# The preparation as pieces of the batches' list schedule, in smaller splits, with the weight sums and a mask on POOL and x among the first loads

## The chip, the cores and the metric

The kernel runs on one core of a Trainium2 chip. Its engines are PE (matrix products and transposes, into PSUM banks), ACT, DVE and POOL (elementwise work) and SP (here only issuing DMAs). Each has its own queue of instructions, carried out in order, and they wait for each other by semaphores. The metric is the device time of the whole program in microseconds.

## What is computed

x is 16 batches of 512 rows and 256 features, adj is one 512x512 matrix for all. Four layers follow one another, each with a residual and a layernorm:

```python
x = _layernorm(x + _L0_gnn_ref(...))   # norm_adj @ (x @ weight); norm_adj = adj scaled by rsqrt(degree) on both sides
x = _layernorm(x + _L1_gnn_ref(...))   # attention, 8 heads, masked where adj == 0; proj; o + layernorm(o)
x = _layernorm(x + _L2_gnn_ref(...))   # 3 steps of a gated unit on adj @ h
x = _layernorm(x + _L3_gnn_ref(...))   # attention, 8 heads, scores + (1 - adj) * -1e9; proj
```

float32 throughout; only the weights, adj and vectors that depend on no batch can be prepared ahead.

## The kernel before

Each float32 operand of a product is held as a high part, rounded to fp32r (ACT writes it), and a low part, the remainder (DVE or POOL writes it); a product is three matmuls on PE, high x low, high x high and low x high (L1226 to L1228, `product`). adj is used transposed (`adjT`), all weights lie in one tensor `W` (HI, LO), of which the first nine blocks of 256 columns ("plain": w0, q1, k1, v1, o1, q3, k3, v3, o3) come straight from memory by way of `raw`, and five ("turned": w3, w4, w5, u3, u5) must be transposed by PE first. w3, w4 and w5 are sums of two halves, w4 has w3 subtracted from it, q1 and q3 are scaled.

Three batches are in flight (`STREAMS`), each with its own buffers `res`, `vh`, `feat`, `qk`. One attention runs at a time, in tiles of 128 queries: scores on PE (L1275), mask and least value on DVE (L1031, `shift`), exponential on ACT (L805), transposes on PE (L1283), a copy to `PT` by ACT or DVE, values on PE (L1298). For it the parts of q and k are copied to `stack` by DMAs (L676).

The order on every engine comes from a planner at build time, the class `Order`: each piece of work has an engine, an assumed duration and lateness (`nominal`), the pieces it comes after, and the PSUM banks that it opens or frees. `run` takes again and again, among the heads of all its queues, the piece with the earliest start, and of equals the one with the longest way to the end (`ways`). The result is one fixed order for each engine, `order.by_engine`; on the chip every engine goes through its own and waits where it must, whatever the planner had assumed.

The preparation is not in that plan: it is written out at the head of each engine's program. SP issues adj, then w3, w4, w5, u3, u5, then the plain weights, then rows and vectors, all of these on one semaphore `raw_loaded`. DVE (L934 to L973) computes the degrees, mask1 (bf16) and mask3 (float32), the low parts of adjT, and after `raw_loaded` the scalings and sums, the bias columns, dinv (the power itself is POOL's, L691), bo, the low part of all plain weights in one instruction (L967) and five low parts of the turned ones (L971). ACT writes the high parts, the plain ones in one instruction (L783). PE transposes adj (L1207), and after DVE's u5 the five weights (L1215), then a small product for bo (L1219). SP waits for the last low part, stores bo to memory (L642), waits for that, and only then takes up the planned order, in which the loads of x for batches 0, 1 and 2 (L658) and the bias row (L653) come first. `raw` lies over `feat` and `qk`, the buffers of the batches; raw w3 and w4 lie in `PT`, w5 in `vh2`, u3 and u5 in `res2`.

A batch then goes: x scaled by dinv (high L833 on ACT, low L1070 on DVE), POOL adds the bias row (L738), two products with adjT ("ax"), two with w0, layernorm n0 (moments on DVE, power on POOL L704, ACT L840), transposes (L1266), q, k, v, stack, attention.

## Time and profile before

| what | us |
|---|---|
| median of 3 runs | 2619.9 |
| lowest and highest | 2617.76, 2620.14 |
| the profiled execution, time | 2621.08 |
| its span in the trace | 2619.3 |

The mean granted clock of PE in the profiled execution was 0.989 of full speed. "Busy" counts the instructions' own time; what an engine stands still for is named as the releaser in brackets. A row of the timeline gives start, duration, engine, line and operation, with neighbours of one kind merged (x4).

### The profile page before, as it was taken

Reading aid. Unit: us, or ns where it says so; the run is one execution under the profiler, and the core shown is the slowest. Engines: PE = TensorE matmul, PEld = TensorE weight load, DVE = VectorE, ACT = ScalarE, POOL = GpSimd, SP = SyncE. Lnnn points to the kernel's source line nnn. Section 1 sums busy time; section 2 is a strip of 40 time slices with the busy share of each in tenths; the row PEclk is TensorE's granted clock in tenths of the full one; section 3 lists DMA queues with packets and bytes.
Section 4 is the critical chain, followed back from the end, with each engine's and each line's share of the span. In section 5 each row is a group of like instructions: output and inputs, shape, how many; then the busy total and the mean of one; then the engine's idle time right before and its main releaser. Section 6 shows DMA issues by size and latency. Waiting matters only on the chain.

```text
span 2619.3 us, 50145 instructions
## 1 busy us (share of the span) xinstructions
PE 2544.9 (97%) x17384; PEld 2048.2 (78%) x17384; DVE 1973.5 (75%) x5487; ACT 1896.5 (72%) x4273; POOL 756.2 (29%) x1081
## 2 busy tenths in 40 slices
PE   4999999999999999999999999999999999999997
PEld 3877777887878888787887878888788887778875
DVE  4867867868687786887868788786887868776776
ACT  3767857769587695867769587695877859575787
POOL 1222242322413223142322413224142232323221
PEclk7999999999999999999999999999999999999999
DMA  3312203122031221302122031221212223021122
GB/s 117 73 27 49 52 20 69 32 61 60 26 70 42 53 51 45 73 22 65 38 54 67 21 76 41 53 52 45 66 29 55 48 51 69 19 51 27 31 63 54
DMA packets 91082, 132.14 MB, mean 50 GB/s; under 512 B 15921, under 2 KB 40146, under 8 KB 90834
## 3 DMA queue, kind: packets, MB, share of 16 engines
q1 hardware_dynamic: 90834, 128.94, 20.7%
q8 instruction: 143, 2.34, 0.4%
q14 instruction: 105, 0.86, 0.1%
HBM read 19.83 MB, written 8.39 MB: 11 GB/s over the span
## 4 chain that ended last, share of the span: by engine, by line
PE 91%; DVE 4%; issue 1%; ACT 1%; POOL 1%; SPq 1%; DMA 0%; DVEq 0%; ACTq 0%; POOLq 0%
PE bank L1226 18%; PE bank L1227 17%; PE bank L1228 17%; PE bank L1283 16%; PE bank L1298 9%; PE bank L1275 8%; PE bank L1303 2%; PE bank L1266 2%; PE bank L1336 1%; DVE probs L1031 1%; SPq L624 1%; DVE vh L1097 0%; ACT probs L805 0%; DVE gate L1008 0%; DVE gate L1132 0%
## 5 line engine op out<-in xcount | busy, mean ns | idle before, releaser
L805 ACT ACTIVATE probs<-probs,few 128x512 f32<-128x512 f32 x1024 | 732.5, 720 | 88.8 <-DVE few L1031 84.4
L1031 DVE CUSTOM_DVE_ANT_0 probs<-bank,mask 128x512 f32<-128x512 f32 x1024 | 677.3, 683 | 58.3 <-PE bank L1283 26.3
L1283 PE MATMUL bank<-ident,probs 128*128 128x128 f32 x4096 | 585.4, 273 | 8.9 <-ACT probs L805 7.1
L1283 PEld LDWEIGHTS bank<-ident,probs 128*128 128x128 f32 x4096 | 484.1, 141 | 92.8 <-issue 27.9
L1275 PE MATMUL bank<-stack 96*128 96x512 f32 x1024 | 415.2, 451 | 1.8 <-DMA stack<-qk 0.7
L814 ACT ACTIVATE PT<-bank 128x512 f32<-128x512 f32 x630 | 354.6, 597 | 51.3 <-PE bank L1303 25.8
L1042 DVE COPY PT<-bank 128x512 f32<-128x512 f32 x394 | 269.0, 688 | 84.7 <-PE bank L1283 46.4
L727 POOL TENSOR_TENSOR feat<-o,feat 128x256 fp32r<-128x256 f32 x128 | 95.2, 744 | 615.1 <-ACT feat L827 606.3
L1226 PE MATMUL bank<-feat,W 128*128 128x512 f32 x640 | 259.9, 406 | 0.0
L1298 PE MATMUL bank<-PT,vh 128*32 128x256 f32 x4096 | 254.8, 383 | 1.1 <-issue 0.7
L840 ACT ACTIVATE res<-res,few 128x256 f32<-128x256 f32 x256 | 139.6, 593 | 156.8 <-POOL few L712 155.0
L1227 PE MATMUL bank<-feat,W 128*128 128x512 f32 x640 | 252.9, 395 | 0.0
L1228 PE MATMUL bank<-feat,W 128*128 128x512 f32 x640 | 252.8, 395 | 0.0
L1226 PE MATMUL bank<-qk,W 128*128 128x512 f32 x576 | 231.3, 402 | 2.9 <-DVE few L1031 1.9
L1226 PE MATMUL bank<-adjT,qk 128*128 128x512 f32 x512 | 208.6, 407 | 24.3 <-DVE qk L1070 15.7
L1228 PE MATMUL bank<-qk,W 128*128 128x512 f32 x576 | 227.7, 395 | 0.0
L1227 PE MATMUL bank<-qk,W 128*128 128x512 f32 x576 | 227.5, 395 | 0.0
L744 POOL TENSOR_TENSOR feat<-gate,feat 128x512 fp32r<-128x512 f32 x96 | 130.1, 1368 | 277.8 <-ACT feat L868 277.7
L1227 PE MATMUL bank<-adjT,qk 128*128 128x512 f32 x512 | 204.8, 400 | 0.0
L1228 PE MATMUL bank<-adjT,qk 128*128 128x512 f32 x512 | 204.2, 399 | 0.0
L794 ACT ACTIVATE qk<-bank 128x512 fp32r<-128x512 f32 x160 | 94.6, 593 | 146.4 <-PE bank L1228 146.3
L805 ACT ACTIVATION_READ_ACCUMULATOR probs<-probs,few 128x1 f32 x1024 | 198.7, 194 | 0.0
(110 smaller groups left out, 4995.6 us busy)
## 6 DMA issues: line engine op xcount, KB each, us to landing
stack<-qk SPq DMA_DIRECT2D x768, 128.0 KB, 2.4
res<-in_x_dram SPq DMA_DIRECT2D x16, 512.0 KB, 3.8
out_dram<-res SPq DMA_DIRECT2D x16, 512.0 KB, 2.9
rows<-bo_sum SPq DMA_DIRECT2D x15, 128.0 KB, 2.9
rows<-in_L_gnn_bias_dram SPq DMA_DIRECT2D x14, 128.0 KB, 2.9
rows<-in_L_gnn_ln_beta_dram SPq DMA_DIRECT2D x14, 128.0 KB, 2.9
PT<-in_adj_dram SPq DMA_DIRECT2D x1, 1024.0 KB, 5.4
PT<-in_L_gnn_w_w_dram SPq DMA_DIRECT2D x2, 512.0 KB, 6.7
```

The costliest lines, as they stand in the source:

```text
L744: i = pool.tensor_tensor(feat[j][:, LO, f, :], src[j][:, f, :], feat[j][:, HI, f, :].bitcast(F32), ALU.subtract)
L805: k = act.activation(p, p, ACT.Exp, bias=least[:, t % P_RING:t % P_RING + 1], scale=-1.0, accum_out=sums[:, grp % 2, q * HG + h:q * HG + h ...
L814: k = act.activation(PT[:, t % PT_RING, :], place("transpose", t)[:, :], ACT.Copy)
L840: k = act.activation(res[j][:, t, :], res[j][:, t, :], ACT.Identity, bias=mv[j][:, t, 0:1], scale=mv[j][:, t, 1:2])
L1031: k = dve.tensor_tensor_reduce(out=probs[:, t % P_RING, :], in0=place("scores", t)[:, :], in1=mask[:, half * QT + q, :], scale=1.0, scalar ...
L1042: k = dve.tensor_copy(PT[:, t % PT_RING, :], place("transpose", t)[:, :])
L1226: pe.matmul(dst, a(HI), b(LO), start=start, stop=False)
L1227: pe.matmul(dst, a(HI), b(HI), start=False, stop=False)
L1228: return pe.matmul(dst, a(LO), b(HI), start=False, stop=stop)
L1275: k = pe.matmul(place("scores", t)[:, :], stack[0:STACKED * HD, 0, h, cs], stack[0:STACKED * HD, 1, h, :], start=True, stop=True)
L1283: k = pe.transpose(place("transpose", t)[:, m * P:(m + 1) * P], probs[:, t % P_RING, m * P:(m + 1) * P], ident[:, :])
L1298: pe.matmul(dst[h * HD:(h + 1) * HD, 0:QH], v_v[j][:, m, c:c + HD], pt_v[:, pt_slots(grp, h), m, :], start=(m == 0), stop=(m == NT - 1))
```

## The change

The preparation becomes pieces of the same plan. New planner entries `("raw", ...)` are SP's loads, each group on a semaphore of its own, in the order adj, x of batch 0, w0, x of batch 1, qkv, the other plain weights, the GRU weights, small vectors, rows; `("prep", engine, ...)` are the steps on PE, ACT, DVE and POOL. The plain weights are split in seven pieces for ACT and DVE. The four sums of weights go from DVE to POOL, as does mask3, which comes after the power. The transposes open PSUM banks as other pieces do. `raw` now lies over `stack` and the head of `PT`, adj one slot further in `PT`, raw w4 in `vh1`. x of batch 2 is loaded once u3 and u5 are transposed (they lie in `res2`). The first stack of batch 0 waits for the whole preparation. The arithmetic is the same.

```diff
+PREP_US = {"deg": 2.65, "mask1": 1.14, "mask3": 5.0, "w3": 1.3, "w4": 1.3, "w4-w3": 1.3, "w5": 1.3, "dinv": 0.1, "pow": 0.8, "q1": 0.34, "q3": 0.34, "u5": 0.35,
+           "cols": 0.6, "bv": 0.6, "bo": 0.35, "hi_qkv1": 1.35, "lo_qkv1": 1.65,
+           "lo_q3": 0.6, "hi_q3": 0.5, "bo_sum": 0.1}
+RAW_US = {"adj": (0.6, 4.6), "w0": (0.6, 2.5), "rows": (1.2, 2.0), "qkv1": (0.6, 3.5), "gru": (3.0, 5.0), "rest": (3.0, 5.0),
+          "small": (5.4, 2.0), "bo_sum": (0.6, 3.0)}
+
...
+    turned = ("w3", "w4", "w5", "u3", "u5")
+    adjs = [f"adj{m}" for m in range(NT)]
+    for name in ("adj", "x0", "w0", "x1", "qkv1", "rest", "gru", "small", "rows"):
+        add("first", "SP", ("load", int(name[1])) if name[0] == "x" else ("raw", name))
+    add("bo_sum", "SP", ("raw", "bo_sum"), ("prep", "DVE", "bo"))
+    for m in range(NT):
+        add(("prep", "PE"), "PE", ("prep", "PE", adjs[m]), ("raw", "adj"), opens=[("adjT", m)])
+        add(("prep", "ACT"), "ACT", ("prep", "ACT", adjs[m]), ("prep", "PE", adjs[m]))
+        add(("prep", "DVE"), "DVE", ("prep", "DVE", adjs[m]), ("prep", "ACT", adjs[m]), frees=[("adjT", m)])
+    add("degrees", "DVE", ("prep", "DVE", "deg"), ("raw", "adj"))
+    add("degrees", "POOL", ("prep", "POOL", "pow"), ("prep", "DVE", "deg"))
+    add("degrees", "DVE", ("prep", "DVE", "dinv"), ("prep", "POOL", "pow"))
+    add("masks", "DVE", ("prep", "DVE", "mask1"), ("raw", "adj"))
+    add("masks_pool", "POOL", ("prep", "POOL", "mask3"), ("prep", "POOL", "pow"))
+    later = ("o1", "q3", "k3", "v3", "o3")
+    for loaded, scaled, name in (("w0", None, "w0"), ("qkv1", "q1", "qkv1"),
+                                 *(("rest", "q3" if name == "q3" else None, name) for name in later)):
+        if scaled:
+            add("plain", "DVE", ("prep", "DVE", scaled), ("raw", loaded))
+        add("plain", "ACT", ("prep", "ACT", f"hi_{name}"), ("raw", loaded), *([("prep", "DVE", scaled)] if scaled else []))
+        add("plain", "DVE", ("prep", "DVE", f"lo_{name}"), ("prep", "ACT", f"hi_{name}"))
+    for name in ("w3", "w4", "w4-w3", "w5"):
+        add("sums", "POOL", ("prep", "POOL", name), ("raw", "gru"))
+    add("sums_dve", "DVE", ("prep", "DVE", "u5"), ("raw", "gru"))
+    for name, ready in zip(turned, (("prep", "POOL", "w3"), ("prep", "POOL", "w4-w3"), ("prep", "POOL", "w5"), ("raw", "gru"),
+                                    ("prep", "DVE", "u5"))):
+        add("turned", "PE", ("prep", "PE", name), ready, opens=[("turn", name)])
+        add(("turned", "ACT"), "ACT", ("prep", "ACT", name), ("prep", "PE", name))
+        add(("turned", "DVE"), "DVE", ("prep", "DVE", f"lo_{name}"), ("prep", "ACT", name), frees=[("turn", name)])
+    add("biases", "DVE", ("prep", "DVE", "cols"), ("raw", "small"), ("raw", "rows"))
+    add("biases", "PE", ("prep", "PE", "bv"), ("raw", "small"), ("raw", "rest"), opens=[("bv", 0)])
+    add("biases", "DVE", ("prep", "DVE", "bo"), ("prep", "PE", "bv"), frees=[("bv", 0)])
+    prepared = [("prep", "DVE", name) for name in ("lo_w0", "lo_qkv1", *(f"lo_{name}" for name in later), "lo_u5", "mask1",
+                                                     "dinv", adjs[-1])]
+    prepared += [("prep", "POOL", "mask3"), ("raw", "bo_sum")]
+
     for n, (what, of) in enumerate(ROWS):
-        add("rows", "SP", ("row", n), *([("pool", ROWS[n - 1][0], b) for b in ROWS[n - 1][1]] if n else []))
+        add("rows", "SP", ("row", n), *([("pool", ROWS[n - 1][0], b) for b in ROWS[n - 1][1]] if n else [("raw", "w0")]),
+            *([("raw", "bo_sum")] if what == "bo" else []))
...
-        add(sp, "SP", ("load", b), *([("store", b - STREAMS)] if b >= STREAMS else []))
+        if b >= 2:
+            add(sp, "SP", ("load", b), ("store", b - STREAMS) if b >= STREAMS else ("prep", "PE", "u5"))
         for t in range(NT):
-            add(act, "ACT", ("act", "scale", b, t), ("load", b))
+            add(act, "ACT", ("act", "scale", b, t), ("load", b), ("prep", "DVE", "dinv"))
             add(dve, "DVE", ("dve", "scale", b, t), ("act", "scale", b, t))
         add(pool, "POOL", ("pool", "scale", b), ("dve", "scale", b, NT - 1), ("row", row_at["scale", b]))
         for f in range(FT):
-            add(pe, "PE", ("pe", "ax", b, f), ("dve", "scale", b, NT - 1), opens=[("ax", b, f)])
+            add(pe, "PE", ("pe", "ax", b, f), ("dve", "scale", b, NT - 1), ("prep", "DVE", adjs[-1]), opens=[("ax", b, f)])
             evacuated(b, ("ax", b), f)
...
-            add(pe, "PE", ("pe", "w0", b, tp), ("dve", "ax", b, FT - 1), opens=[("w0", b, tp)])
+            add(pe, "PE", ("pe", "w0", b, tp), ("dve", "ax", b, FT - 1), ("prep", "DVE", "lo_w0"),
+                opens=[("w0", b, tp)])
...
+                        *(prepared if layer == 1 and b == 0 else []), *([("stt", last_of_head(first, h))] if first else []))
...
+                add(pe, "PE", ("pe", "v", b, layer, tp), ("prep", "PE", "w4"), ("prep", "PE", "w5"), opens=[("v", b, layer, tp)])
...
+        raw = nc.alloc_sbuf_tensor_at("raw", [P, FT, PLAIN], F32, offset=at)
         early = PT[:, :, :].rearrange("p r c -> p (r c)")
-        adj_n = early[:, 0:NT * N].rearrange("p (t m) -> p t m", t=NT)
-        raw_w = [v.rearrange("p (o c) -> p o c", o=FT)
-                 for v in (early[:, 4 * N:6 * N], early[:, 6 * N:8 * N], vh[2][:, :])]
+        adj_n = early[:, N:(1 + NT) * N].rearrange("p (t m) -> p t m", t=NT)
+        raw_w = [v.rearrange("p (o c) -> p o c", o=FT) for v in (early[:, 5 * N:7 * N], vh[1][:, :], vh[2][:, :])]
...
+            def raw_loads(what):
+                if what == "adj":
+                    sp.dma_start(adj_n, adj.rearrange("(t p) m -> p t m", p=P)).then_inc(adj_loaded, 16)
+                elif what == "w0":
+                    weights([("w0", w0)], w0_loaded)
+                elif what == "qkv1":
+                    weights([("q1", wqkv)], qkv1_loaded)
+                elif what == "rest":
+                    weights([("o1", wproj), ("q3", wq), ("k3", wk), ("v3", wv), ("o3", wo)], rest_loaded)
+                elif what == "gru":
+                    for to, w in zip(raw_w, (w3, w4, w5)):
+                        sp.dma_start(to, w.rearrange("(o p) c -> p o c", p=P)).then_inc(gru_loaded, 16)
+                    for to, w in zip(raw_u, (u3, u5)):
+                        sp.dma_start(to, w.rearrange("(o p) c -> p o c", p=P)).then_inc(gru_loaded, 16)
+                elif what == "rows":
+                    for i, v in enumerate((gamma, bproj)):
+                        sp.dma_start(rows[:, 1 + i, :], v.partition_broadcast(P)).then_inc(rows_loaded, 16)
+                elif what == "bo_sum":
+                    sp.wait_ge(prep_dve.sem, prep_dve.at("bo"))
+                    sp.dma_start(bo_sum[:, :], raw_bo[0:1, :]).then_inc(bo_stored, 16)
+                else:
+                    sp.dma_start(raw_bo, bo.partition_broadcast(HD)).then_inc(small_loaded, 16)
+                    small(cols, (bq, bk, w3b, w4b, w5b), small_loaded)
+                    small(raw_cols, (u3b, u5b, bv), small_loaded)
...
+                    if n == 2:
+                        sp.wait_ge(bo_stored, 16)
...
+                    if b == 2:
+
+                        wait_full(sp, "turn", "u3")
+                        wait_full(sp, "turn", "u5")
...
+                    if layer == 1 and b == 0:
+
+                        sp.wait_ge(prep_dve.sem, len(prep_dve.steps))
+                        sp.wait_ge(prep_pool.sem, len(prep_pool.steps))
+                        sp.wait_ge(bo_stored, 16)
...
+            def weight_sums(what):
+                pool.wait_ge(gru_loaded, 16 * 5)
+                if what == "w4-w3":
+
+                    pool.wait_ge(prep_pool.sem, prep_pool.at("w4"))
+                    i = pool.tensor_tensor(raw_w[1][:, :, 0:D], raw_w[1][:, :, 0:D], raw_w[0][:, :, 0:D], ALU.subtract)
+                else:
+                    w = raw_w[turned.index(what)]
+                    i = pool.tensor_tensor(w[:, :, 0:D], w[:, :, 0:D], w[:, :, D:2 * D], ALU.add)
+                prep_pool.raised_by(i, what)
+
+            def third_mask():
+                pool.wait_ge(adj_loaded, 16)
+                i = pool.tensor_scalar(mask3[:, :, :], adj_n, 1.0, -FAR, ALU.subtract, ALU.mult)
+                prep_pool.raised_by(i, "mask3")
+
+            def powers():
+                pool.wait_ge(prep_dve.sem, prep_dve.at("some"))
+                prep_pool.raised_by(pool.tensor_tensor(deg[:, 2, :], deg[:, 1, :], power[:, :], ALU.pow), "pow")
...
+            def prepare(what):
+                if what in adjs:
+                    m = adjs.index(what)
+                    wait_full(act, "adjT", m)
+                    k = act.activation(adjT[:, HI, m, :], place("adjT", m)[:, :], ACT.Copy)
+                elif what in turned:
+                    wait_full(act, "turn", what)
+                    c = col[what]
+                    k = act.activation(W[:, HI, :, c:c + D], place("turn", what)[:, :].rearrange("p (k c) -> p k c", k=FT),
+                                       ACT.Copy)
+                else:
+                    if what == "hi_w0":
+                        act.wait_ge(w0_loaded, 16)
+                    elif what == "hi_qkv1":
+                        act.wait_ge(qkv1_loaded, 16)
+                        act.wait_ge(prep_dve.sem, prep_dve.at("q1"))
+                    else:
+                        act.wait_ge(rest_loaded, 16 * 5)
+                        if what == "hi_q3":
+                            act.wait_ge(prep_dve.sem, prep_dve.at("q3"))
+                    c = plain[what[3:]]
+                    k = act.activation(W[:, HI, :, c], raw[:, :, c], ACT.Copy)
+                prep_act.raised_by(k, what)
...
+                elif what in ("q1", "q3"):
+                    if what == "q1":
+                        dve.wait_ge(qkv1_loaded, 16)
+                    else:
+                        dve.wait_ge(rest_loaded, 16 * 5)
+                    c = col[what]
+                    prep(dve.tensor_scalar(raw[:, :, c:c + D], raw[:, :, c:c + D], -SCALE, None, ALU.mult), what)
+                elif what[:3] == "lo_" and what[3:] in plain:
+                    dve.wait_ge(prep_act.sem, prep_act.at("hi" + what[2:]))
+                    c = plain[what[3:]]
+                    prep(dve.tensor_tensor(W[:, LO, :, c], raw[:, :, c], W[:, HI, :, c].bitcast(F32), ALU.subtract), what)
+                elif what == "u5":
+                    dve.wait_ge(gru_loaded, 16 * 5)
+                    prep(dve.tensor_scalar(raw_u[1], raw_u[1], 0.5, None, ALU.mult), what)
...
+                    wait_free(pe, "turn", what)
+                    if what == "u3":
+                        pe.wait_ge(gru_loaded, 16 * 5)
+                    elif what == "u5":
+                        pe.wait_ge(prep_dve.sem, prep_dve.at("u5"))
+                    else:
+                        pe.wait_ge(prep_pool.sem, prep_pool.at("w4-w3" if what == "w4" else what))
...
+                    if f == 0 and b < STREAMS:
+                        pe.wait_ge(prep_dve.sem, prep_dve.all(adjs))
...
```

## Rows read from the trace of the kernel before

**Rows 1.** Busy time, share of span and instructions, the page's first part.

```profile
PE 2544.9 (97%) x17384; PEld 2048.2 (78%) x17384; DVE 1973.5 (75%) x5487; ACT 1896.5 (72%) x4273; POOL 756.2 (29%) x1081
```

**Rows 2.** Stretches: length, busy us (instructions) by engine, granted clock, DMA share, GB/s.

```profile
0.00:46.70 46.70, 9.92 (x40) 7.96 (x41) 21.12 (x33) 12.30 (x15) 2.98 (x9) 0.68 0.47 149
46.70:78.80 32.10, 32.09 (x173) 27.71 (x174) 19.04 (x53) 13.88 (x28) 15.00 (x20) 0.93 0.17 45
...
120.00:300.00 180.00, 170.49 (x1160) 132.35 (x1159) 131.68 (x382) 135.21 (x311) 49.97 (x72) 1.00 0.20 44
300.00:2500.00 2200.00, 2188.46 (x14836) 1766.37 (x14836) 1676.87 (x4627) 1609.23 (x3615) 653.55 (x917) 1.00 0.20 48
2500.00:2619.30 119.30, 102.78 (x846) 80.01 (x844) 89.09 (x285) 90.94 (x220) 27.70 (x53) 0.95 0.23 58
```

The busy columns of such a row are PE, PE's weight loads, DVE, ACT and POOL.

**Rows 3.** Timeline of the preparation: start, duration, engine, line, operation.

```profile
6.19 2.29 DVE L934 TENSOR_REDUCE probs<-PT 128x4 f32<-128x2048 f32 x1 [6.19 <-DMA PT<-in_adj_dram]
...
6.30 3.65 PE L1207 MATMUL bank<-ident,PT 128*128 128x128 f32 x16 [6.30 <-DMA PT<-in_adj_dram]
...
8.84 2.22 POOL L691 TENSOR_TENSOR probs<-probs,few 128x4 f32<-128x4 f32 x1 [7.30 <-DVE probs L937]
...
9.80 1.22 DVE L939 TENSOR_SCALAR mask<-PT 128x2048 f32<-128x2048 f32 x1
...
21.19 0.76 DVE L947 TENSOR_SCALAR raw<-raw 128x512 f32<-128x512 f32 x2 [7.78 <-DMA probs<-in_L_gnn_bv_dram]
...
31.40 4.94 DVE L967 TENSOR_TENSOR W<-raw,W 128x4608 fp32r<-128x4608 f32 x1
...
46.71 0.76 PE L1226 MATMUL bank<-adjT,qk 128*128 128x512 f32 x1 [15.68 <-DVE qk L1070]
```

**Rows 4.** Wo's load: its issue (timeline), and the median from issue to landing.

```profile
9.97 1.08 SPq L624 DMA_DIRECT2D raw<-in_L_gnn_Wo_dram  x1
...
raw<-in_L_gnn_Wo_dram SPq DMA_DIRECT2D x1, 256.0 KB, 8.2
```

**Rows 5.** POOL's groups by line and shape: busy us, mean ns of one.

```profile
L738 POOL TENSOR_TENSOR res<-res,rows 128x1024 f32<-128x1024 f32 x48 | 115.5, 2407 | 233.7 <-DVE feat L998 139.2 <-DVE qk L1070 58.7 <-DMA rows<-in_L_gnn_bias_dram 35.7
L744 POOL TENSOR_TENSOR feat<-vh,feat 128x512 fp32r<-128x512 f32 x64 | 81.9, 1300 | 119.7 <-ACT feat L890 118.8
...
L704 POOL TENSOR_TENSOR few<-few 128x2 f32<-128x2 f32 x160 | 118.8, 743 | 2.7
```

**Rows 6.** DVE beside POOL: two timeline rows, then two lines' min/median/max ns.

```profile
48.59 0.80 DVE L1070 SCALAR_TENSOR_TENSOR qk<-res,few,qk 128x256 fp32r<-128x256 f32 x1 [2.03 <-ACT qk L833]
...
46.74 2.37 POOL L738 TENSOR_TENSOR res<-res,rows 128x1024 f32<-128x1024 f32 x1 [35.68 <-DMA rows<-in_L_gnn_bias_dram]
...
L1070 DVE SCALAR_TENSOR_TENSOR qk<-res,few,qk x64: 450/484/799, 44.9 to 2271.0; 128x256 fp32r<-128x256 f32 x64
...
L1123 DVE SCALAR_TENSOR_TENSOR gate<-gate,vh x96: 640/683/2895, 169.8 to 2507.6; 128x512 f32<-128x512 f32 x96
```

**Rows 7.** Clock: two stretches (columns as Rows 2), and ACT's second evacuation (timeline).

```profile
26.00:28.00 2.00, 2.00 (x11) 2.00 (x10) 0.00 (x0) 1.50 (x4) 0.00 (x0) 0.50 0.00 0
...
51.00:52.00 1.00, 1.00 (x5) 0.78 (x5) 1.00 (x4) 1.00 (x4) 0.00 (x0) 0.86 0.00 0
...
54.65 0.60 ACT L794 ACTIVATE feat<-bank 128x512 fp32r<-128x512 f32 x1 [1.85 <-PE bank L1228]
```

**Rows 8.** From w0 of batch 0 to the first scores, timeline of SP and PE.

```profile
57.55 0.35 SPq L653 DMA_DIRECT2D rows<-in_L_gnn_ln_beta_dram  x1
...
59.94 0.28 PE L1228 MATMUL bank<-W,feat 128*128 128x256 f32 x1
...
65.66 1.03 PE L1266 MATMUL bank<-ident,res 128*128 128x128 f32 x8
...
73.68 50.61 SPq L676 DMA_DIRECT2D stack<-qk  x36
...
78.53 0.71 PE L1275 MATMUL bank<-stack 96*128 96x512 f32 x2
```

More of the change, by code:

```diff
@@ L38, in at, with all @@
         return it * len(self.steps) + self.place[step] + 1
+    def all(self, steps):
+        return max(self.at(step) for step in steps)
     def raised_by(self, instruction, step):
@@ new lines, in weights, with small @@
+            def weights(names, loaded):
+                for name, w in names:
+                    c = col[name]
+                    sp.dma_start(raw[:, :, c:c + w.shape[1]], w.rearrange("(k p) c -> p k c", p=P)).then_inc(loaded, 16)
+            def small(to, vectors, loaded):
+                for i, v in enumerate(vectors):
+                    sp.dma_start(to[:, i, :], v.rearrange("(f p) -> p f", p=P),
+                                 allow_slow_non_contiguous=True).then_inc(loaded, 16)
+            def raw_loads(what):
[22 more added lines that the diff above has]
+                    small(raw_cols, (u3b, u5b, bv), small_loaded)
```

218 lines of the change are left out of this document (108 added, 110 removed).

## The prediction

> **What bounds the kernel now.** Read the busy totals first [rows 1]: PE is busy 97% of the span, DVE 75%, ACT 72%, POOL 29%. So this is a PE kernel, and only time in which PE has nothing to do, or runs at the low clock, can be had. Then read where that time lies [rows 2]. Of the 2619.3 us, PE is busy 2544.9, so it idles 74.4. The first 46.7 us hold 36.8 of them (46.70 − 9.92). The stretch to 78.8 us holds none, 120 to 300 holds 9.5, the 2200 us up to 2500 hold only 11.5, and the last 119 us 16.5. Half of all idle time is the preparation, in 2% of the span. The timeline of the preparation shows why [rows 3]: everything is in series. PE turns adj (6.30, 3.65 us) and is done; DVE waits until 21.19 for the last of 23 small and large loads, SP's single semaphore standing at the very last vector; then it scales and sums the weights, PE turns them, DVE writes the low parts (31.40, 4.94 us, then five pieces). Only then does SP issue the store of bo and, behind it, the first load of x; the first real product starts at 46.71. From there PE is without a gap to the first scores at 78.53 [rows 2, 8].
>
> **The change, part by part.**
>
> *Loads.* adj still lands at 6.2 us. In the kernel before, 4.25 MB more had landed when Wo's load ended, about 8.2 us after its issue at 9.97, so at 18.2 us [rows 4]: 4.25/12.0 = 0.354 MB/us. In the new order (adj, x0, w0, x1, qkv, the rest, the five GRU weights, the first bias row) that rate gives x0 (0.5 MB) at 7.6, w0 (0.25) at 8.3, x1 at 9.7, qkv (0.75) at 11.8, the rest (1.25) at 15.3, the GRU weights (2.0) at 21, the row (0.13) at 21.4. The row's place behind the GRU weights follows from the planner's ranks: when SP comes free at its 6.0, the loads' chain (the weights' and then the small vectors' way) is longer than the row's.
>
> *First product.* The planner believes w0 loaded at its 4.3 us and adj at 5.2, so it puts hi_w0 first on ACT and lo_w0 first on DVE. On the chip adj is there at 6.2 and w0 at 8.3: the degree sum waits behind lo_w0. hi_w0 8.3 to 8.95 (0.60, as ACT's other 128x512 pieces [rows 7]), lo_w0 to 9.7 (0.68, as DVE's median for that size [rows 6]), sum to 12.0 (2.29) and two small steps to 12.2 [rows 3]. The low parts of adjT, 0.68 each, go on; POOL's power took 2.22 us, but ended as DVE's mask3 did, at 11.06 against 11.02; elsewhere the same kind is 0.74 [rows 3, 5]. I take 0.8: power at 13.1. dinv follows the third adjT piece, at 14.3. The fourth piece (0.68) and q1 (0.4, half of the 0.76 at 21.19) take DVE to 15.4, then come the low parts of x0, four in 1.7 (from 44.9 to the product's 46.71 in before [rows 3, 6]), which ACT's parts run ahead of; undisturbed they end at 17.1, and at 17.2 the product starts, 29.5 us earlier than now.
>
> *mask3 on POOL.* This is what disturbs it. Nothing of this shape and operation is on POOL in the trace. From above: a sum of two tensors, 128x1024, takes 2.40, twice that is 4.8 [rows 5]. From below: DVE's own 1.22. I take 4.8, the nearest row being an elementwise POOL operation of half the size. It then runs 13.1 to 17.9. What matters is who waits for it. A DVE operation with two SBUF tensors that meets a POOL one is stretched: the low part of x starting at 48.59 took 0.80 instead of 0.484 while POOL's 46.74 + 2.37 ended at 49.11, and over the kernel one gate operation took 2895 ns where the median is 683 [rows 6]; the excess, 2.2 us, is nearly one POOL operation of 2.40. The power above is the opposite case, POOL held by DVE. So q1 and the low parts of x0 wait until 17.9 and the product starts at 17.9 + 0.4 + 1.7 = 20.0. With the lower price for mask3 it is 17.2.
> The Trainium skill (SBUF — State Buffer, "SBUF: two separate sides") says that VectorE and GpSimd share a port pair as an exclusive lock for a whole instruction, taken by VectorE operations with two SBUF inputs or in a 2-port mode; by that rule reads from PSUM go on. The rows above agree with it. It speaks against moving work from DVE to POOL here: by it the 2.8 us between 17.2 and 20.0 stand, without it the sum would be 2.8 us better.
>
> *PE's ledger.* Idle before: 36.8. Idle after, up to the first product: 6.3 + (20.0 − 9.95) = 16.4 (13.6 with the cheap mask). Clock: all PE work between 20 and 46.7 us, the weight transposes and bv, is 9.92 − 3.65 = 6.3 us at the granted 0.50, the level of 1.2 GHz [rows 2, 3, 7]. Behind products that run at 2.4 GHz it needs half, which gives 3.1 back. The first products of b0 start at the low clock in both kernels (up at 51 to 52, 4.5 us after the start) [rows 7]: no difference. So the ceiling of the gain is 36.8 − 16.4 + 3.1 = 23.5 us, less the new waits.
>
> *New waits of PE, whose queue is fixed.* (a) w3's transposes stand in PE's order behind the two products of b0, which end at 27.9 (from 46.71 to the second one's evacuation at 54.65 it is 7.9 [rows 3, 7]). They need POOL: mask3, then the bias of b0 (2.40, not before its row at 21.4 and not before the low parts of x0), then w3 (1.30) [rows 5]. In clear air that is 25.1; but DVE has q1, x0's parts, mask1, lo_qkv1, u5, x1's parts and more, about 8 us that contend, in one run from 17.9 to 26. POOL gets in late: w3 is ready between 25 and 30. Wait 0 to 2, taken 1.5. (b) w4−w3 and w5 follow 2.6 and 3.9 us later, behind which PE has a product of b1 and w0 of b0: 0 to 2, taken 0.5. (c) b2 can't be loaded before u3 and u5 are turned, at about 38, and so starts at 44; until then PE lives on b0 and b1 alone. In before, nearly six us lie between the end of w0 and the first transposes of n0 (59.94 to 65.66), filled by b1 and b2 [rows 8]. Taken 2, from 0 to 5. (d) DVE: in before it works 21.1 + 19.0 = 40.2 us to 78.8; 4.0 of it go (mask3 1.22, four sums of 0.68), 36 remain between 9 and the new start of attention, besides POOL's 17 us of contending work (mask3 4.8, three biases 7.2, four sums 5.2) against DVE's 12 of the same kind. DVE is thus near full until attention starts. Taken 2, from 0 to 6. Sum 6, from 0 to 15.
>
> *The rest, each with one answer.* ACT's and DVE's splits of the plain weights cost a start of some 0.1 to 0.2 us a piece at a guess from the shortest rows, six pieces more on each, beside idle ACT time and inside term (d). The stacks of b0 wait for the whole preparation and for bo's store; from the steps above all low parts are done by 38 to 40 and bo by 36, and b0's k by about 49, so this wait is covered by 10 us; if it is not, attention waits that much longer. SP has "beta", which waits for the bias of b2, ahead of these stacks; in before it went out at 57.55 against 73.68 for the stacks [rows 8]; now some 46 against 49: covered by 3. The body (2200 us, 11.5 idle) does the same work from a new plan: the order shifts, by ±4 at a guess from the 9.5 + 11.5 + 16.5 that such patterns leave idle.
>
> **Sum.** 23.5 − 6 = 17.5 us. The profiled execution took 2621.1 (span 2619.3 and 1.8 around it), so 2603.6; the median of the runs, 2619.9, is 1.2 lower, so 2602.4, as a forecast 2602 us. Scores should then start near 54 instead of 78.5; that is more than 17.5 earlier since some of b1's and b2's work is done after it.
>
> **The rivals.**
> 1. *POOL and DVE hardly meet.* mask3 is near DVE's price, the product starts at 17.2, waits are 2: gain 36.8 − 13.6 + 3.1 − 2 = 24.3, 2596 us. For it: the planner's order leaves gaps on both; against it: the stretched rows. The Trainium skill (GPSIMD Engine Reference, "Engine selection") calls a one-input operation on GpSimd roughly line-rate, which would make mask3 cheap and so lead to this rival's time; no row of this case shows it.
> 2. *The queues stand.* The new waits reach their upper end, 15: gain 23.5 − 15 = 8.5, 2611 us. For it: four queues now wait on each other with loads 7 to 9 us later than the planner assumed (GRU weights at 21 for its 14). It decides once POOL's w3 is later than about 32.
> 3. *Slower: the plan of the body gets worse.* The list schedule is one greedy run; with b2 some 20 us behind b0 where all three were level, the batches may line up so that their serial gates coincide. It decides when the body's idle share grows from 0.5% to over 1.6% (11.5 + 24 us); one pattern that costs 1.9 us more in each of 13 rounds does it, and at 6 us net on the wrong side it gives 2626. Against it: PE's work is the same and the backlog of three batches is deep.
> 4. *The change does not do what it says*: x0 is early but a late piece stands ahead of it in one queue (u5, or a sum, waiting for the GRU weights at 21). Then the product starts at 21.5 + 1.7 or later: 3 us less, inside my range.
>
> **How the numbers follow.** Forecast with case 4: 0.68, 2602. Case 1: 0.15, 2596. Case 2: 0.12, 2611. Case 3: 0.05, 2626. The range takes in cases 1 and 2 with 2 to 3 us of the plan's shift beyond them on either side: 2593 to 2613. A measurement of this kernel can tell about 0.2%, 5.2 us, from no change: 2614.7 to 2625.1. Case 2 with a bad plan gives the most of "same": 0.08. Slower 0.04, faster 0.88.
>
> **What would show it.** Right: PE's idle time before its first adj product 16 us, that product at 20; low parts of x0 on DVE waiting for POOL's mask3; first scores near 54; PE idle of 300 to 2500 us within 4 of 11.5. Wrong: the product beyond 25 (a load or a DVE piece ahead of it), mask3 far from 4.8, PE waits of over 3 us for POOL's sums, or a body with more idle time.

## The result, and the profile after

The changed kernel takes 2607.25 us (median of 5, 2605.07 to 2608.49), the kernel before 2619.31 beside it (2617.76 to 2620.14): ratio 0.9953 [0.9942, 0.9964], 12.1 us or 0.46% faster. The forecast was 2602, its range 2593 to 2613. The profiled execution took 2605.07 with a span of 2603.3, against 2621.08 and 2619.3: 16.0 us less. It was the fastest of its five, while the profiled one of before lies above its own median, which is why the two executions stand further apart than the medians.

Stretches of after (length, busy us of PE, PE's weight loads, DVE, ACT, POOL, then granted clock), to be held against [rows 1, 2]:

```profile
PE 2541.7 (98%) x17384; PEld 2045.9 (79%) x17384; DVE 1978.7 (76%) x5491; ACT 1895.5 (73%) x4278; POOL 771.8 (30%) x1086
...
0.00:46.70 46.70, 22.64 (x105) 18.29 (x106) 35.22 (x59) 19.55 (x37) 26.20 (x24) 0.96 0.52 161
46.70:78.80 32.10, 32.10 (x214) 26.99 (x213) 22.82 (x72) 20.72 (x47) 8.43 (x12) 1.00 0.34 77
...
120.00:300.00 180.00, 172.06 (x1179) 132.44 (x1178) 130.93 (x374) 131.74 (x301) 46.44 (x66) 1.00 0.21 46
300.00:2500.00 2200.00, 2186.87 (x14802) 1765.37 (x14801) 1675.32 (x4618) 1608.73 (x3614) 655.65 (x919) 1.00 0.20 48
2500.00:2603.30 103.30, 86.77 (x739) 67.90 (x737) 76.68 (x257) 77.85 (x191) 23.75 (x49) 0.96 0.25 62
```

Read them as a ledger of PE's idle time. In the first 46.7 us it falls from 36.78 to 24.06 (46.70 − 22.64), 12.7 less. From 120 us to 2500 it is 7.94 + 13.13 = 21.07, against 9.51 + 11.54 = 21.05, and the last stretch holds 16.5 in both: nothing won or lost there. PE's busy time falls by 3.2 (2544.9 to 2541.7) with the same 17384 matmuls. Some 2.6 of that is the weight transposes and bv: 6.3 us of PE at the granted 0.50 in before [rows 7], 3.7 in after (30.35 to 32.00 and 39.02 to 41.05), where the median transpose takes 0.27 us for 0.42. The other 0.6 is a balance of stretches at the low level (1.2 GHz) elsewhere, as far as the rows show it. After has one more: PE stands 2.70 us before 34.70, and from 35.8 to 39.2 its 128x256 matmuls take 0.41 us for 0.28 (granted 0.52). It has less of it behind the first product, whose 0.63 us matmuls (0.40 later) end 3.2 us after its start for 4.4 in before, and less in the body (one stretch of some 7 us near 350 in before, of some 3 near 334 in after). The granted clock of the first row, 0.96, leaves those first matmuls out: they ran as slowly as at the recorded 0.50 in before. 12.7 + 3.2 is the 16.0.

The timeline of after's preparation (start, duration, engine, line, operation, and in brackets the idle time before it and its releaser):

```profile
6.04 3.65 PE L1345 MATMUL bank<-ident,PT 128*128 128x128 f32 x16 [6.04 <-DMA PT<-in_adj_dram]
...
8.28 0.63 ACT L908 ACTIVATE W<-raw 128x512 fp32r<-128x512 f32 x1 [6.28 <-DMA raw<-in_L_gnn_weight_dram]
...
9.55 2.28 DVE L1059 TENSOR_REDUCE probs<-PT 128x4 f32<-128x2048 f32 x1
...
12.19 1.03 POOL L794 TENSOR_TENSOR probs<-probs,few 128x4 f32<-128x4 f32 x1 [10.66 <-DVE probs L1062]
...
13.30 7.12 POOL L789 TENSOR_SCALAR mask<-PT 128x2048 f32<-128x2048 f32 x1
13.81 4.03 DVE L1065 TENSOR_TENSOR few<-probs 128x4 f32<-128x4 f32 x1
...
18.36 2.33 DVE L1080 TENSOR_SCALAR raw<-raw 128x512 f32<-128x512 f32 x1
...
20.62 1.66 DVE L1202 SCALAR_TENSOR_TENSOR qk<-res,few,qk 128x256 fp32r<-128x256 f32 x4
...
22.19 1.22 DVE L1068 TENSOR_SCALAR mask<-PT 128x2048 bf16<-128x2048 f32 x1
...
22.33 0.79 PE L1373 MATMUL bank<-adjT,qk 128*128 128x512 f32 x1 [12.64 <-DVE qk L1202]
22.36 6.25 POOL L841 TENSOR_TENSOR res<-res,rows 128x1024 f32<-128x1024 f32 x1 [1.94 <-DVE qk L1202]
...
25.94 0.41 DVE L1087 TENSOR_SCALAR res<-res 128x512 f32<-128x512 f32 x1
...
28.14 2.71 DVE L1084 TENSOR_TENSOR W<-raw,W 128x512 fp32r<-128x512 f32 x2
...
28.58 1.72 POOL L784 TENSOR_TENSOR PT<-PT 128x512 f32<-128x512 f32 x1
...
30.35 0.66 PE L1367 MATMUL bank<-ident,PT 128*128 128x128 f32 x4 [0.69 <-POOL PT L784]
30.77 1.23 DVE L1097 TENSOR_SCALAR few<-few 128x2 f32<-128x2 f32 x1
...
33.92 0.68 DVE L1130 TENSOR_TENSOR feat<-bank,feat 128x512 fp32r<-128x512 f32 x1
...
34.70 0.36 PE L1373 MATMUL bank<-W,feat 128*128 128x256 f32 x1 [2.70 <-DVE W L1084]
...
39.02 1.15 PE L1367 MATMUL bank<-ident,vh 128*128 128x128 f32 x8
...
40.01 1.04 PE L1367 MATMUL bank<-ident,res 128*128 128x128 f32 x8
...
58.82 0.86 PE L1422 MATMUL bank<-stack 96*128 96x512 f32 x3
```

Three things are to be seen. First, mask3 takes POOL 7.12 us, and dinv (L1065), four values a partition, 4.03 beside it; q1 (L1080) takes 2.33 where half of the 0.76 in [rows 3] would do. Second, POOL's bias of batch 0 takes 6.25 for the 2.40 of [rows 5]: DVE goes from mask1 at 22.19 without a pause through low parts and scalings of the weights to 26.35, and POOL's sum ends 2.26 us behind that, at 28.61. Third, the two trade places: DVE's scaling of a bias column (L1097) takes 1.23 beside POOL's sums, and PE, at 34.70, has stood 2.70 us for the last low part of ax (the 33.92 row, which ends at 34.60; the profile names the low part of weights just before it). The first product starts at 22.33 for 46.71 in before, the first scores at 58.82 for 78.53 [rows 8].

### The profile page after: what moved, and what is told of

Its sections match the earlier page's. It is cut to its first block, busy times and chain, and to the rows that moved or that the text cites. A ratio compares the mean times of both kernels' runs of the same rounds, so it can differ in the third digit from the quotient of the medians.

```text
span 2603.3 us, 50181 instructions
## 1 busy us (share of the span) xinstructions
PE 2541.7 (98%) x17384; PEld 2045.9 (79%) x17384; DVE 1978.7 (76%) x5491; ACT 1895.5 (73%) x4278; POOL 771.8 (30%) x1086
## 4 chain that ended last, share of the span: by engine, by line
PE 92%; DVE 5%; issue 1%; ACT 1%; POOL 1%; DMA 0%; SPq 0%; DVEq 0%; ACTq 0%; POOLq 0%
PE bank L1373 18%; PE bank L1375 18%; PE bank L1374 18%; PE bank L1430 16%; PE bank L1445 9%; PE bank L1422 8%; PE bank L1450 2%; PE bank L1413 2%; PE bank L1483 1%; DVE probs L1163 1%; DVE vh L1229 0%; DVE gate L1140 0%; DVE gate L1264 0%; DVE PT L1174 0%; DVE res L1233 0%
## 5 line engine op out<-in xcount | busy, mean ns | idle before, releaser
L1373 PE MATMUL bank<-adjT,qk 128*128 128x512 f32 x512 | 207.2, 405 | 21.4 <-DVE qk L1202 12.6
```

What stands on the lines that cost most here:

```text
L1373: pe.matmul(dst, a(HI), b(LO), start=start, stop=False)
```

## The experiments

Four readings are to be told apart. The lock-out: mask3 on POOL, and DVE and POOL holding each other, cost what is missing. The order: the planner takes the loads for earlier than they are and puts the first bias row late. Early x: that is what brings most of the gain. The plan: a difference comes from the redrawn order of the body. Each variant is made from the changed kernel unless it says "before". Times are medians of 5 runs (4, 10 or 1 where said), each with its ratio to the kernel before on the same chip. The runs were made on several chips, on which before had medians from 2618.5 to 2619.6, and an interval is some 3 us to either side. So a variant that differs from after by 3 or 4 us is not told from it by the time alone, and its trace has to carry the reading; clear of after's [0.9942, 0.9964] are the kernel with the landings told and the row early, and the two kernels with everything mended and x first; mask3 on ACT touches it.

### mask3 on DVE, or on POOL behind the sums

```diff
-    add("masks_pool", "POOL", ("prep", "POOL", "mask3"), ("prep", "POOL", "pow"))
+    add("masks", "DVE", ("prep", "DVE", "mask3"), ("raw", "adj"))
```

> The changed kernel, but mask3 is made on DVE again, as a piece of the plan behind mask1. Theory P (DVE and POOL block each other on SBUF): dinv loses its 4.03 us beside POOL's 7.12 us mask3 and ends near 14.2, q1 its 2.33, the first adj product starts at 17 to 18 instead of 22.33, and POOL's bias of b0 and its sums come earlier; mask3 on DVE is 1.22 us. PE idle time to 46.7 us falls by 3 to 5 us from 24.1, the time by 3 to 5 us against the changed kernel (ratio to before near 0.994). Theory Q (the stretch has another cause, such as loads landing at 13 to 20 us): dinv stays at 4 us, product at 22, no gain.

The plan has mask3 at 1.14 us there. 2603.86 us, 0.9943 [0.9930, 0.9955]. Timeline of this kernel:

```profile
14.08 0.15 DVE L1065 TENSOR_TENSOR few<-probs 128x4 f32<-128x4 f32 x1
...
16.80 0.80 PE L1376 MATMUL bank<-adjT,qk 128*128 128x512 f32 x1 [7.04 <-DVE qk L1205]
...
21.97 2.39 POOL L841 TENSOR_TENSOR res<-res,rows 128x1024 f32<-128x1024 f32 x1 [8.48 <-DMA rows<-in_L_gnn_bias_dram]
...
31.80 1.20 DVE L1071 TENSOR_SCALAR mask<-PT 128x2048 f32<-128x2048 f32 x1
```

dinv is back at 0.15 us and the product 5.5 us earlier, so mask3 did hold them. But the median fell by only 3.4: the bias of batch 0 still starts at 21.97, now for its row, which lands then, and the sums of weights stand behind it.

```diff
-    add("masks_pool", "POOL", ("prep", "POOL", "mask3"), ("prep", "POOL", "pow"))
...
     for name in ("w3", "w4", "w4-w3", "w5"):
         add("sums", "POOL", ("prep", "POOL", name), ("raw", "gru"))
+    add("sums", "POOL", ("prep", "POOL", "mask3"), ("raw", "adj"))
```

> The changed kernel, but POOL makes mask3 behind the four sums of weights. Theory P: dinv 0.1 to 0.2 us, first product at 17 to 18 as without mask3 on POOL; the blocking moves to 28 to 36 us, where it meets DVE's low parts and POOL's own bias and power for b0 stand behind mask3, so that first scores come no earlier than in the changed kernel (58.9) and the time is within 3 us of it. Theory Q: product at 22.

2604.63 us, 0.9947 [0.9934, 0.9959]. Timeline, and PE's waits in the first 60 us (total, times, longest):

```profile
30.97 7.12 POOL L789 TENSOR_SCALAR mask<-PT 128x2048 f32<-128x2048 f32 x1
31.81 4.22 DVE L1084 TENSOR_TENSOR W<-raw,W 128x512 fp32r<-128x512 f32 x1
```

```profile
PE bank L1373 <- DVE qk L1202: 6.8, 1, 6.8
...
PE bank L1373 <- issue: 5.9, 1, 5.9
```

The product starts at 16.78 again, but the hold moves with the mask: a low part of 0.68 takes 4.22. PE stands 5.9 us in one piece, before the first product of batch 1 at 42.80, whose low parts of x DVE has behind all that; at most 3.5 of them (4.22 − 0.68) can be the hold's. In the preparation nothing is won, as the ledger below shows: 0.6 us less idle time, and 3.2 us more of PE's busy time.

### mask3 on POOL alone, in before

```diff
+            prep_pool.raised_by(pool.tensor_scalar(mask3[:, :, :], adj_n, 1.0, -FAR, ALU.subtract, ALU.mult), "mask3")
...
-            prep(dve.tensor_scalar(mask3[:, :, :], adj_n, 1.0, -FAR, ALU.subtract, ALU.mult), "mask3")
```

> The kernel before, with mask3 alone moved to POOL, behind the power; DVE has nothing to do from about 12.5 to 21 us. It prices mask3 on POOL with DVE mostly away: theory P says 5 us or less there (7.12 in the changed kernel being partly blocking), so the power ends at about 10.9 with mask1, mask3 runs to 16, and nothing waits for it: time as before, 2617 to 2621. If it takes 7 us here too, 7 is its own price.

2620.25 us, one run, not told from before (2617.79 to 2620.19 beside it). Timeline:

```profile
10.94 7.12 POOL L692 TENSOR_SCALAR mask<-PT 128x2048 f32<-128x2048 f32 x1
```

The same 7.12 us in another kernel, at another time, where 5 or less had been expected: a duration of the operation, not a stretching. Where DVE waits for loads anyway, one run shows no cost of it.

### The planner told the true landing of w0

```diff
-RAW_US = {"adj": (0.6, 4.6), "w0": (0.6, 2.5), ...
+RAW_US = {"adj": (0.6, 4.6), "w0": (0.6, 6.5), ...
```

> The changed kernel with one number of the planner changed: w0 is assumed to land at 8.3 us, as it does, instead of 4.3. DVE then starts with the degree sum at 6.1 instead of 9.55 and takes lo_w0 after adjT. If the wait for w0 is a term of its own, power, dinv and the first product come 3 us earlier (19.3 instead of 22.33) and the time falls by 2 to 3 us; if the mask on POOL or x0's landing (7.6) absorbs it, less than 1 us.

2604.13 us, 0.9946 [0.9932, 0.9959]. Timeline:

```profile
10.05 7.12 POOL L789 TENSOR_SCALAR mask<-PT 128x2048 f32<-128x2048 f32 x1
10.56 4.02 DVE L1065 TENSOR_TENSOR few<-probs 128x4 f32<-128x4 f32 x1
...
15.71 1.66 DVE L1202 SCALAR_TENSOR_TENSOR qk<-res,few,qk 128x256 fp32r<-128x256 f32 x4
...
17.42 0.80 PE L1373 MATMUL bank<-adjT,qk 128*128 128x512 f32 x1 [7.37 <-DVE qk L1202]
```

With the degrees summed ahead of lo_w0, dinv, mask3 and the product all move up, the product from 22.33 to 17.42, with mask3 as it was. The rows also show what the hold is: dinv is released 4.5 us into mask3 (14.58 − 10.05), as in after (17.84 − 13.30 = 4.54), and the four low parts of x then run at full speed beside the rest of it, from 15.71 to 17.37.

### x last: in after, and first in before

```diff
-    for name in ("adj", "x0", "w0", "x1", "qkv1", "rest", "gru", "small", "rows"):
+    for name in ("adj", "w0", "qkv1", "rest", "gru", "small", "rows", "x0", "x1"):
```

> The changed kernel, but x of batches 0 and 1 is loaded behind all weights, vectors and rows. It tells the value of the early x apart from that of the pieces in the plan. x0 then lands at 24 to 25 us, the first adj product starts at 27 to 29 instead of 22.33, but the weight transposes (2.5 us of PE) come before it. Theory S (the gain is from the preparation no longer being in series): PE idle time to 46.7 us is only 2 to 4 us more than the changed kernel's 24.1, and 8 to 11 of the 12 us of gain remain. Theory X (x among the first loads is what counts): less than half of the gain remains, 2613 us or more.

2606.99 us, 0.9953 [0.9940, 0.9965]: as fast as after. Timeline and first stretch:

```profile
33.73 0.76 PE L1373 MATMUL bank<-adjT,qk 128*128 128x512 f32 x1 [3.67 <-issue]
...
0.00:46.70 46.70, 23.34 (x101) 18.62 (x102) 34.85 (x49) 17.42 (x32) 23.86 (x17) 0.78 0.52 164
```

The product starts 11.4 us later than in after, and PE has done nearly the same by 46.7 (101 matmuls for 105), since the weight transposes come ahead of that product, from 20.62 on, and behind it PE has no waits. The other way round, x of batches 0 and 1 loaded behind adj in before:

```diff
+            for b in (0, 1):
+                sp.dma_start(res[b][:, :, :], x_v[b]).then_inc(x_loaded[b], 16)
             for i, w in enumerate((w3, w4, w5)):
...
+                    if b >= 2:
+                        sp.dma_start(res[b % STREAMS][:, :, :], x_v[b]).then_inc(x_loaded[b % STREAMS], 16)
```

> The kernel before with one part alone: x of batches 0 and 1 is loaded behind adj (the preparation stays as it was, in series, with one semaphore). The last vector lands 2.5 to 3 us later (1 MB more in front, at 0.35 MB/us), which pushes DVE's start from 21.19 to 22 to 24, and x is there when the preparation ends, which saves the 3.9 us between x's issue at 40.48 and ACT's start at 44.34 and the store of bo ahead of it. Net gain 1 to 4 us: x early is worth little while the preparation is in series.

2617.74 us (10 runs), 0.9996 [0.9986, 1.0005]: the product starts at 43.00, no difference in time that can be told. Early x falls as the source of the gain in the kernel as changed: what it gained it gained by no longer doing the preparation in series. Which part of that does it was not tried: the group semaphores, the splits of the plain weights and the interleaving with the batches were never undone one at a time.

### The sums back on DVE

```diff
-        add("sums", "POOL", ("prep", "POOL", name), ("raw", "gru"))
+        add("sums", "DVE", ("prep", "DVE", name), ("raw", "gru"))
```

> The changed kernel with one part undone: the four sums of weights are made by DVE again, as pieces of the plan (0.68 us each for 1.26 to 1.79 on POOL). First product unchanged at 22.3. Theory P and a full DVE: DVE is busy 35.2 of the first 46.7 us and gets 2.7 more, but loses the waits beside POOL's sums (near 3 us between 28 and 35), so that the time is within 2 us of the changed kernel; the planner also moves b1 behind b0's v, which can cost 2 us more. A gain of over 3 us would say that the sums on POOL were a mistake, a loss of over 3 that DVE's own time is the bound of the start.

The plan has them at 0.62 us each. 2603.74 us, 0.9940 [0.9927, 0.9952], 3.5 us under after; the two profiled executions are only 1.3 apart in span. PE's idle time of the first 120 us hardly moves (23.85 for 24.06); it is behind 120 us that 3.0 us are missing, of which PE's busy time takes back 1.9. POOL's bias of batch 0 still takes 6.17 us. That points to a shift of the plan and not to the sums, and the same edit in the mended kernel below, worth 0.2, agrees.

### Both causes taken away, and one at a time

All: mask3 on ACT, which computes the same values as FAR − FAR · adj, the first bias row loaded behind qkv, and the planner told the landings that the trace shows.

```diff
+                if what == "mask3":
+                    act.wait_ge(adj_loaded, 16)
+                    act.wait_ge(prep_pool.sem, prep_pool.at("far"))
+                    k = act.activation(mask3[:, :, :], adj_n, ACT.Identity, bias=far[:, 0:1], scale=-FAR)
...
+RAW_US = {"adj": (0.6, 5.6), "w0": (0.6, 6.5), "rows": (1.2, 8.0), "qkv1": (0.6, 9.0), "gru": (3.0, 12.2), "rest": (3.0, 10.3),
+          "small": (5.4, 8.5), "bo_sum": (0.6, 3.0)}
...
+    for name in ("adj", "x0", "w0", "x1", "qkv1", "row0", "rest", "gru", "small", "rows"):
```

> The changed kernel with everything that the last runs point to: mask3 on ACT (activation with scale -1e9 and bias 1e9, about 2 us, ACT has its own way to SBUF and is idle then), the first bias row loaded ahead of the last eleven weights, and the planner told the landings that the trace shows (adj 6.2, w0 8.3, qkv 12, rest 17, GRU weights 22, vectors 24 us). Theory P plus the queue order: first product at 14 to 15 us, POOL's bias of b0 at 17 instead of 22 to 28, b1's first product ahead of w3's transposes, PE idle to 46.7 us near 15 to 17 instead of 24.1, time 6 to 9 us under the changed kernel, near 2599. If PE is then held by the GRU weights' landing at 22 us and the sums behind it, the idle time only moves, and the time is within 3 us of the mask on DVE (2603.9).

2594.94 us (4 runs), 0.9905 [0.9892, 0.9919]: 12.3 us under after, and more than the 6 to 9 that had been expected. Timeline and first stretch:

```profile
5.93 2.00 ACT L893 ACTIVATE mask<-PT,few 128x2048 f32<-128x2048 f32 x1 [3.54 <-DMA PT<-in_adj_dram]
...
14.13 0.79 PE L1379 MATMUL bank<-adjT,qk 128*128 128x512 f32 x1 [4.44 <-DVE qk L1208]
14.16 3.10 POOL L843 TENSOR_TENSOR res<-res,rows 128x1024 f32<-128x1024 f32 x1 [3.65 <-DVE qk L1208]
...
14.60 0.42 DVE L1086 TENSOR_SCALAR raw<-raw 128x512 f32<-128x512 f32 x1
...
14.94 3.79 DVE L1208 SCALAR_TENSOR_TENSOR qk<-res,few,qk 128x256 fp32r<-128x256 f32 x4
...
0.00:46.70 46.70, 32.71 (x167) 27.05 (x168) 38.69 (x82) 25.65 (x45) 22.19 (x29) 1.00 0.53 162
```

PE idles 14.0 us in the preparation instead of 24.1. The lock-out is not gone: the bias of batch 0 and the low parts of batch 1 hold each other (3.10 for 2.40, 3.79 for 1.66).

The mask on ACT alone:

> The changed kernel with mask3 alone moved, to ACT instead of POOL (planner: 1.95 us). No DVE or POOL time for it at all. Theory P: as with mask3 on DVE (2603.9, first product at 16.8) or 1 to 2 us better, since DVE has 1.22 us less. What stays are the bias row at 22 us and the order of b1 behind n0, so that it stays 7 us or more above the kernel with all three (2594.9): 2602 to 2605.

2601.38 us, 0.9929 [0.9917, 0.9942], a little better than expected; the product at 16.76. Landings told and the row early, mask3 still on POOL, told as 7.1:

> The kernel with all three edits less the first: mask3 stays on POOL, told to the planner at its measured 7.1 us; the bias row comes early and the planner knows the landings. mask3 on POOL runs from 10 to 17 us and holds dinv by 4 us, so that the first product is at 17 to 18; the bias of b0 follows mask3 at 17 and b1's products stand early in PE's order. If the landings and the row carry most of the 12.3 us between the changed kernel and the one with all three, this gives 2597 to 2600; if the mask does, 2603 or more.

2599.69 us, 0.9922 [0.9909, 0.9936]; the product at 17.26. The two give 5.9 and 7.6 by medians, 13.5 in all, and together 12.3; but of the 5.9 the ledger below gives the preparation only 0.7. All of it, with the sums on DVE:

> The kernel with all three edits, and the four sums on DVE as well: POOL has only the power, the bias adds and the layernorms' small steps. In the changed kernel the sums on DVE gave 3 us. DVE is busy 38.7 of the first 46.7 us here and gets 2.7 more, but nothing meets POOL between 22 and 29 us (about 5 us of stretched DVE operations there). Theory P: 0 to 3 us better than 2594.9; theory D (DVE's own time now bounds the start): 1 to 3 us worse.

2594.79 us (4 runs), 0.9905 [0.9892, 0.9919], as without: the four sums are worth nothing on either engine. And all of it with x last again, the planner told so; the bias row goes late with it. Against the kernel with all:

```diff
-    for name in ("adj", "x0", "w0", "x1", "qkv1", "row0", "rest", "gru", "small", "rows"):
+    for name in ("adj", "w0", "qkv1", "rest", "gru", "small", "rows", "x0", "row0", "x1"):
```

> The kernel with all three edits, but with x of batches 0 and 1 behind all other loads (the planner told so). In the changed kernel the place of x made no difference (2607.0 against 2607.3), since its first product waited for POOL and DVE anyway. Here those waits are gone, and the first product would start at 27 to 28 instead of 12.4 us: 6 to 10 us worse than 2594.9, 2601 to 2605. If it is again the same, the early x is worth nothing in any order, and the gain is the pieces' and the planner's alone.

2606.15 us, 0.9947 [0.9935, 0.9960]: 11.2 us more, where 6 to 10 had been expected. Timeline and first stretch:

```profile
28.69 0.77 PE L1379 MATMUL bank<-adjT,qk 128*128 128x512 f32 x1 [3.18 <-issue]
...
0.00:46.70 46.70, 25.89 (x112) 20.12 (x112) 31.63 (x60) 20.66 (x36) 16.04 (x23) 0.82 0.51 161
```

Early x brings nothing that can be told while the low parts behind it are locked out and the row is late, and 11 us once they are not, of which 2 lie behind 120 us.

### The ledger of all of them

From the stretches of each profiled execution: PE's idle time before and behind 120 us, and its busy time. Medians beside it.

| kernel | median | first product | idle to 120 | idle behind 120 | PE busy | span |
|---|---|---|---|---|---|---|
| before | 2619.3 | 46.71 | 36.8 | 37.6 | 2544.9 | 2619.3 |
| after | 2607.3 | 22.33 | 24.1 | 37.6 | 2541.7 | 2603.3 |
| mask3 on DVE | 2603.9 | 16.80 | 20.1 | 36.2 | 2542.7 | 2599.0 |
| mask3 behind the sums | 2604.6 | 16.78 | 23.5 | 35.8 | 2544.9 | 2604.2 |
| w0 told | 2604.1 | 17.42 | 21.5 | 37.4 | 2543.4 | 2602.3 |
| x last | 2607.0 | 33.73 | 25.0 | 35.7 | 2543.1 | 2603.9 |
| sums on DVE | 2603.7 | 22.48 | 23.9 | 34.6 | 2543.6 | 2602.0 |
| mask3 on ACT | 2601.4 | 16.76 | 21.4 | 34.2 | 2543.7 | 2599.3 |
| landings told, row early | 2599.7 | 17.26 | 18.8 | 37.3 | 2541.8 | 2597.9 |
| all | 2594.9 | 14.13 | 15.7 | 35.6 | 2541.5 | 2592.8 |
| all, sums on DVE | 2594.8 | 14.20 | 14.8 | 35.5 | 2542.7 | 2593.0 |
| all, x last | 2606.2 | 28.69 | 23.1 | 37.7 | 2543.6 | 2604.4 |

Every edit at the head of the list redraws the plan of all that follows, and idle time behind 120 us then lies anywhere from 34.2 to 37.7. That it is the plan is argued, not shown: before with x first has the order of before and 36.1 for 37.6 there, and five runs of after alone spread over 3.4 us. A difference of 3 us between two variants may be that alone, as with the sums on DVE; so is 3.4 of what "mask3 on ACT" has over after, and 1.8 for "mask3 behind the sums". The preparation is read in the column to 120, less what PE's busy time loses, mostly by its clock. Against after, the mask off POOL saves 3.9 us of idle time on DVE and 2.7 on ACT, of which 1.0 and 2.0 are lost again; the landings and the row save 5.3 and lose 0.2; both save 8.4 and lose nothing. So the landings and the row are the larger part by either measure, and the mask's own part lies between 0.7 and 2.9 us. Early x saves 7.4 in the mended kernel, and 2.1 of busy time besides; in the changed one only 1.0 and 1.5, which its luckier body takes back.

## Why the prediction was right, and where it was off

**The place of the gain** was right: all of it is in the preparation, with PE, not DVE, as the bound. The time lies inside the range, but the gain is 12.1 us where the sum had 17.5. Of its own signs, "mask3 far from 4.8" stood on the list for wrong and came true; on the list for right, the first product (22.33 for 20), the idle time before it (18.7 for 16) and the first scores (58.82 for 54) came late, and it was dinv and q1, not the low parts of x, that waited for mask3.

**Loads.** Right: hi_w0 starts at 8.28 (8.3 forecast), and the bias row of batch 0 is there at 21.97 in the kernel with mask3 on DVE (21.4). lo_w0 ahead of the degrees: they start at 9.55 (9.7). The kernel that tells the planner w0's landing shows that this order alone cost 4.9 us of the product's start (22.33 − 17.42), and 2.6 of idle time.

**mask3: the term that was mis-sized.** The step went by the nearest row, a two-tensor sum on POOL, with 4.8 us at most. It is 7.12, outside the range that was given. The form of the wait was also a little other: dinv was to pass at 14.3 and q1 to meet the mask; dinv itself met it at 13.81. The product came at 22.33 for 20.0. Two bounds were wrong together: nothing made two tensor operands an upper bound for a one-tensor operation with two arithmetic steps. The product of the kernels with mask3 on DVE or ACT starts at 16.8 for the 17.2 foreseen with a cheap mask. The Trainium skill (GPSIMD Engine Reference, "Engine selection") calls a one-input operation there roughly line-rate; the 7.12 us for 2048 elements a partition, against DVE's 1.22 and ACT's 2.00 for the same mask, speak against it here.

**The hold.** The step that DVE waits out mask3 was half right. It waits 4.5 us of the 7.12 with dinv, whose operands both lie in SBUF; then the low parts of x run free, as the rows of the kernel with w0 told show; but q1, one tensor in and out, at 18.36, ends at 20.69 where mask3 ends at 20.42. The Trainium skill (SBUF — State Buffer, "SBUF: two separate sides") says of the port lock that it lasts the full instruction. For dinv the rows differ from that, for q1 they agree.

**PE's ledger.** Idle up to the first product is 6.04 + (22.33 − 9.69) = 18.7, for 16.4, the 2.3 of mask3. The clock gave 3.2 (3.1), and that this is so near is luck in part: the transposes and bv gave 2.6, and "no difference" behind the first product was a balance, 1.2 us less of the low level there and 3.4 us of it new from 35.8 on. New waits: 24.06 − 18.7 = 5.4, for 6. So 36.8 − 18.7 + 3.2 − 5.4 = 15.9, the 16.0 of the two executions, where 17.5 was forecast.

Inside those waits the shares were off. (a) w3 waited 0.7 (1.5), at 30.35 for 25 to 30: the bias ahead of it took 6.25, as was feared. (b) and (d): the one large wait, 2.7, is w0's product behind DVE's run of low parts and columns, the fullness of DVE that had been priced at 2. (c) There was no wait for batch 2 as such, but 1.8 us at the transposes of batch 0's n0, from 41 us on, which the first product of batch 1 stands behind:

```profile
PE bank L1413 <- ACT res L961: 1.8, 3, 1.4
...
44.72 2.40 POOL L841 TENSOR_TENSOR res<-res,rows 128x1024 f32<-128x1024 f32 x1 [2.00 <-DVE qk L1202]
44.74 0.47 PE L1373 MATMUL bank<-adjT,qk 128*128 128x512 f32 x1
```

The first line is PE's wait, the others are from the timeline: DVE finishes the low parts of x of batch 1 only at 44.6, since the plan has them that late. The prediction had that product right behind w3, near 30; this step was wrong. The first scores are at 58.82 and not near 54, though PE has no gap from 46.7 to 120, so that this delay itself costs nothing.

**The body** was to shift by up to 4 either way: 300 to 2500 holds 13.1 for 11.5, 120 to 300 holds 7.9 for 9.5, net 0. The spread over all variants, everything behind 120 us, is 3.5 us.

**From span to median.** 5.2 us lie between 2602 and 2607.25. 1.5 are the gain that was missing (16.0 for 17.5), 0.4 the rounding to 2602. The other 3.4 are not in the profile: the forecast took the median 1.2 below the profiled execution, as in before, and it is 2.2 above it.

**The rivals.** Queues that stand (2611) gave the right sort of wait, POOL at 6.25 for 2.40, but w3 was ready at 30.3 and not at 32. POOL and DVE hardly meeting (2596) is what the version with all mended comes to, 2594.9, but only with the mask off POOL and the plan told the landings. The slower body did not come.

**Stretched, or shut out?** The hold of POOL by DVE can be read more closely than above. In four kernels POOL's sum of 2.40 us took 6.25, 6.17 (sums on DVE), 3.63 (w0 told) and 3.10 (all), and each time it ended 2.2 to 2.3 us behind the end of a DVE operation: 28.61 behind 26.35, 28.68 behind 26.43, 25.70 behind 23.45, 17.26 behind 15.02. So it ran at its own speed, and the rest of its duration was waiting to be let in. In after and with the sums on DVE it got in when DVE had nothing ready, with w0 told when DVE came to an operation that reads a PSUM bank, and with all mended ahead of a low part of x, which then took 2.6 us for 0.47. Not settled: why that low part let POOL in and the low parts of the weights at 23.33 in after did not. It would take other orders of DVE's low parts against one and the same bias.

## What to carry to other kernels

Moving work between engines is priced from a row of that operation on that engine, or its range stays open upwards; and its place matters as much, since POOL and DVE hold each other; in after a POOL sum stood 3.9 us until DVE paused. A plan that assumes loads too early puts late pieces ahead of ready ones in a fixed queue: feed it the landings that the trace shows (here 7.6 us together with an early bias row, and with the mask on ACT 12.3), and look at all of a plan's idle time before a few us are put down to the edit.

## What the runs showed of the hardware

- A two-step tensor-with-scalars operation, 128x2048 float32, takes 7.12 us on POOL in all seven kernels that have it there, 2.00 on ACT and 1.22 on DVE.
- Beside it, a DVE operation with two SBUF tensors that starts 0.5 us later ends 4.5 us after the start of POOL's, in five kernels (after, w0 told, x last, sums on DVE, landings told); another with one tensor, 128x512 float32, ends 0.3 us behind POOL's end (after, x last, sums on DVE: 2.33 us for 0.42). The 4.22 us of a low part in the kernel with the mask behind the sums ends 5.1 us after the mask's start, of which 0.68 are its own.
- Beside DVE's runs one POOL sum took 6.25 us for 2.40, and in the mended version 3.10, while four low parts beside it took 3.79 for 1.66. Its end lies 2.2 to 2.3 us behind the end of a DVE operation each time: it is kept out and then runs at its own speed.
- PE's clock fell to the low level at 35.8, 1.1 us after PE had taken up work again from a stand of 2.70 us, and was back at 39.2.
